# A transformer block with two layer norms on one core: a step of the second norm moved to GpSimd, two weight loads moved in the transfer queue, all work orders written anew

## The reference, cut to what matters

```
x: (4, 512, 128) fp32; 16 heads of 8; hidden width 512
qkv = x @ qkv_w.T + qkv_b            # per head: q, k, v of 8 each
attn = softmax(q @ k.T / sqrt(8)) @ v, for each batch and head
a = attn @ fc_w.T + fc_b + x
x1 = layernorm(x + a)                # (x - mean) / sqrt(var + 1e-5)
h = silu((x1 @ w1.T) * s1) * ((x1 @ w2.T) * s2)
h = gelu((h @ h1.T) * hs1);  h = gelu((h @ h2.T) * hs2)
out = layernorm(x1 + (h @ w3.T) * s3)
```

## Time and profile before

| | us |
|---|---|
| median of 3 runs | 313.34 (312.37 to 314.75) |
| the profiled execution's own time | 313.6 |
| its span, first to last instruction | 311.8 |
| busy: TensorE, VectorE | 290.1, 249.6 |
| busy: ScalarE, GpSimd | 241.4, 143.4 |

### The profile page before, as it was taken

One profiled execution on the slowest core, in us unless ns is written; L12 is line 12 of the kernel. 1 busy time (PEld: TensorE's weight loads), 2 busy tenths in 40 slices (PEclk: granted clock), 3 DMA queues, 4 the chain that ended last, 5 costly groups with the idle time before them and its releaser, 6 DMA issues.

```text
span 311.8 us, 6746 instructions
## 1 busy us (share of the span) xinstructions
PE 290.1 (93%) x2337; PEld 167.9 (54%) x2337; DVE 249.6 (80%) x561; ACT 241.4 (77%) x458; POOL 143.4 (46%) x255
## 2 busy tenths in 40 slices
PE   8959699999999999999999999998999999999991
PEld 8733254456555546353444363454556568558980
DVE  0669779998989999798899868538998784658993
ACT  2744588898979998999999888989886896984440
POOL 5162679514628991606149816707493290000101
PEclk9979899999999999999999999999999999999996
DMA  5687410045641004403610034450100000010011
GB/s 156 192 149 166 151 37 5 4 65 72 107 68 35 4 0 69 71 5 47 93 52 4 2 55 85 67 78 10 34 4 3 2 3 2 2 36 0 3 34 38
DMA packets 20276, 15.67 MB, mean 50 GB/s; under 512 B 2945, under 2 KB 19090, under 8 KB 20242
## 3 DMA queue, kind: packets, MB, share of 16 engines
q1 hardware_dynamic: 20242, 15.22, 24.9%
HBM read 5.51 MB, written 1.05 MB: 21 GB/s over the span
## 4 chain that ended last, share of the span: by engine, by line
PE 65%; DVE 12%; ACT 8%; SPq 5%; issue 4%; DMA 3%; POOL 0%; POOLq 0%; DVEq 0%; ACTq 0%
PE bank L484 23%; PE bank L524 14%; PE bank L495 8%; PE bank L506 8%; DVE negmax L879 7%; SPq L382 4%; ACT prob L735 4%; PE bank L466 2%; PE bank L548 2%; DMA stack<-mT 2%; PE bank L477 2%; DMA stack<-parts 1%; PE bank L578 1%; PE bank L459 1%; PE bank L565 1%
## 5 line engine op out<-in xcount | busy, mean ns | idle before, releaser
L879 DVE TENSOR_REDUCE negmax<-bank 128x1 f32<-128x512 f32 x256 | 159.8, 682 | 29.9 <-PE bank L495 29.4
L735 ACT ACTIVATE prob<-bank 128x512 f32<-128x512 f32 x256 | 134.0, 618 | 9.1 <-PE bank L506 8.0
L484 PE MATMUL bank<-act,hT 128*128 128x256 f32 (+1 forms) x384 | 71.0, 329 | 0.3 <-DVE negmax L879 0.2
L524 PE MATMUL bank<-prob,v_sb 128*32 128x256 f32 (+1 forms) x768 | 67.4, 458 | 1.2 <-DVE negmax L879 0.9
L484 PEld LDWEIGHTS bank<-act,hT 128*128 128x128 f32 x384 | 55.2, 189 | 11.6 <-issue 3.7
L495 PE MATMUL bank<-stack 64*128 64x512 bf16 x256 | 56.8, 385 | 4.5 <-DMA stack<-parts 3.2
L506 PE MATMUL bank<-stack 64*128 64x256 bf16 (+1 forms) x384 | 55.1, 309 | 3.6 <-DMA stack<-mT 2.8
L802 ACT ACTIVATE h_nat<-bank,hs_all 128x256 f32<-128x256 f32 (+1 forms) x48 | 25.0, 548 | 20.2 <-PE bank L484 19.9
L506 PEld LDWEIGHTS bank<-stack 64*128 64x128 bf16 x384 | 19.6, 94 | 32.1 <-issue 13.5
L524 PEld LDWEIGHTS bank<-prob,v_sb 128*32 128x32 f32 x768 | 21.7, 109 | 26.9 <-issue 16.9
L495 PEld LDWEIGHTS bank<-stack 64*128 64x128 bf16 x256 | 15.9, 94 | 34.3 <-issue 19.7
(11 more groups left out here) (119 smaller groups left out, 357.3 us busy)
## 6 DMA issues: line engine op xcount, KB each, us to landing
stack<-parts SPq DMA_DIRECT2D x64, 128.0 KB, 3.9
x_in<-in_L_attn_x_dram SPq DMA_DIRECT2D x4, 256.0 KB, 3.5
h_nat<-in_L_ffn_h_w_dram SPq DMA_DIRECT2D x1, 1024.0 KB, 7.8
work<-in_L_ffn_h_w_dram SPq DMA_DIRECT2D x1, 1024.0 KB, 6.3
res<-in_L_attn_x_dram SPq DMA_DIRECT2D x4, 256.0 KB, 3.4
work<-in_L_ffn_w_w_dram SPq DMA_DIRECT2D x2, 256.0 KB, 3.4
out_dram<-y SPq DMA_DIRECT2D x4, 128.0 KB, 2.9
out_dram<-y SPq DMA_DIRECT2D x2, 256.0 KB, 2.3
```

The source lines that it names most:

```text
L484: mm = nc.tensor.matmul(dst, w, v, start=first and n == 0, stop=last and n == len(pairs) - 1)
L524: last = nc.tensor.matmul(space("P", pfirst)[at:at + VW, 0:w], v_sb[b % 2][:, kt, of:of + VW], prob[:, t % NP, c * w:(c + 1) * w], start=k ...
L735: nc.scalar.activation(prob[:, n % NP, :], space("T", n)[:, :], ACT.Exp, scale=SCALE).then_inc(emptied("T", n), 1)
L879: nc.vector.tensor_reduce(negmax[:, g % 2, col:col + 1], space("S", n)[:, :], AX.X, ALU.max, negate=True).then_inc(emptied("S", n), 1)
```

## The change

1. `LN_STEPS` is 4: the normalization is a token of its own, `n1` or `n2`, in the function `normalize`, which either VectorE or GpSimd can run. The table `NORM` puts the second norm's normalization of units 0 to 3 on GpSimd (four `n2` tokens, 12 instructions) and leaves that of units 4 and 5, and all of the first norm, on VectorE. `x1_ok` and `y_ok` become one semaphore for each engine (`until_norm`). The residual adds get waits on them.
2. `SP_ORDER`: the second `mrow` comes right behind the batch-0 transfers; `l3` and the second `lh` follow it, instead of preceding it. `xres` of batch 0 moves behind the fifth `mrow`, `xin` of batch 2 behind the sixth. The batch-0 transfers are in another order among themselves (pair 2 completes with the sixth transfer, not the eighth, pair 4 with the thirteenth, not the tenth).
3. `PE_ORDER`: five `K` instead of nine before the first `x`; the total stays 30, and five now stand at the very end. `wt` 3 comes behind the first eight `S`, where it stood ahead of them, `wt` 5 behind the twenty-second, where it stood behind the eighth. `wt` 7 to 9 come ahead of the ninth `T`, where they came behind it, and `Y` of unit 4 comes behind the first `W` of unit 5.
4. `POOL_ORDER`: `xr` of batches 0 and 1 come later (batch 1's behind the twelfth `m`, where it stood behind the eighth), all `n2` are new. `DVE_ORDER`: the last `lo` of a batch's operands moves ahead by some tokens for batch 3; all of unit 4's second norm moves behind unit 5's last split. `r` gets a wait on `qk_lo`. A `lo` branch is added for GpSimd, but no token of `POOL_ORDER` uses it. `ACT_ORDER` follows the others.

```diff
 SP_ORDER = """
 lw lh xin vb
-zk zq zk zq*4 zk*6 mrow zq*3 l3 lh mrow xres mrow more xin mrow*2 spread mrow spread*2 xin spread mrow xres mrow*2 spread*2 mrow*2 spread*2 mrow xres
-out mrow spread*2 mrow spread*2 mrow out xres mrow*3 out*4"""
+zk zq*2 zk zq zk*3 zq zk*3 zq mrow zq*3 mrow lh l3 mrow more mrow*2 xres spread mrow xin spread xin spread*2 mrow xres mrow*2 spread*2 mrow spread
+mrow spread mrow out mrow xres spread*2 mrow spread*2 mrow out xres mrow*3 out*4"""
 PE_ORDER = """
-K:0 K:1 K:2 K:3 K:4 K:5 K:6 K:7 K:0 x:1 wq:2 q:3 q:4 K:5 wf:6 K:7 wt:0 wt:1 K:2 K:5 K:3 K:7 K:4 K:2 v:5 wt:3 K:7 x:6 wt:4 S:0 S:2 S:1 S:7 S:3 S:5 S:0
+K:0 K:1 K:2 K:3 K:4 x:5 wq:6 q:7 q:0 K:1 K:2 K:3 wt:4 K:5 K:6 wt:1 K:7 v:2 K:3 K:0 K:5 K:6 wf:7 wt:4 x:1 S:3 S:0 S:5 S:6 S:2 S:7 S:1 S:4 wt:3 wt:0 K:5
...
-H*3 X:5 K:0 H*2 H:7 A:2 A:3 B*2 H A:4 B H A:1 B H*5 H:0 H*7 H:5623 H*7 W:7 H W*3 H H:4105 H*2 Y:6 H*7 K:2 K:3 K:7 W:6 W*3 K:4 Y:1"""
+B A:5 B A:6 B H*2 A:2 H*5 H:0 B H*7 H:4715 H*8 W:3 H H:6024 W*2 H*9 W W:7 Y:1 W*3 Y:5 K:6 K:0 K:2 K:3 K:4"""
 DVE_ORDER = """
...
-gh*4 l0 gl*4 gh gl gh*2 gl*2 gh l2 gl l2*3 gh gl gh*2 gl gh gl*2 l2*7"""
+gh gl*2 gh gl*2 gh*2 gl*2 gh*2 gl*2 l2*8 n2*2"""
 POOL_ORDER = """
...
-db h0 l0 m xr gh*3 gl gh gl*3 m gh*4 gl*4 p1 m xr h0*2 l0 h0*2 l0*3 m p2 gh*3 gl gh gl*3 m p1*2 p2*3"""
+l0 h0 m h0 u l0*2 h0 l0 xr p2 n2 m gh*3 gl gh gl*3 m gh gl gh*3 gl*3 p1 m xr h0*3 l0*3 h0 l0 m gh*2 gl*2 gh*2 gl*2 m p1 p2 n2 p1 p2 n2 p2*2"""
@@ -102,7 +102,7 @@
     TWO_ONES = float(np.array([0x3F803F80], np.uint32).view(np.float32)[0])
     WT = 3 + 2 * NK
     NP = 16
-    LN_STEPS = 5
+    LN_STEPS = 4
 
     UNITS = [(0, 0, 2), (0, 2, 2), (1, 0, NT), (2, 0, NT), (3, 0, 2), (3, 2, 2)]
     NU = len(UNITS)
@@ -110,6 +110,7 @@
               4), (3, 4, 4), (3, 8, 4), (3, 12, 4), (4, 0, 8), (4, 8, 8), (5, 0, 8), (5, 8, 8)]
     GATE_DVE = {3, 4, 5}
     SPLIT0 = [0, 0, 0, 0, 1, 1]
+    NORM = [(1, 0), (1, 0), (1, 0), (1, 0), (1, 1), (1, 1)]
     SPLIT_G = [(0, 0), (0, 0), (0, 0), (0, 1), (1, 1), (1, 1)]
     DIRECT = {(4, 0), (4, 1), (5, 0), (5, 1)}
     INNER_K = {5}
@@ -139,6 +140,7 @@
     P_AFTER = [max(j for j, o in enumerate(P_OG) if o == og) + 1 for og in range(NO * NU)]
     GATE_POOL = [(u, k) for u in range(NU) if u not in GATE_DVE for k in range(NK)]
     GATE_VEC = [(u, k) for u in range(NU) if u in GATE_DVE for k in range(NK)]
+    ON_N = [[[u for u in range(NU) if NORM[u][i] == e] for e in range(2)] for i in range(2)]
     ON_0 = [[(u, k) for u in range(NU) for k in range(NK) if SPLIT0[u] == e] for e in range(2)]
     ON_G = [[(u, y, k) for u in range(NU) for y in range(2) for k in range(NK) if SPLIT_G[u][y] == e] for e in range(2)]
     H_PIECES = []
@@ -263,7 +265,7 @@
         lo_max, ps_low = sem("lo_max"), sem("ps_low")
         res2, resb = sem("res2"), sem("resb")
         rs_ok, ln_step = ([sem(f"{n}{i}") for i in range(2)] for n in ("rs_ok", "ln_step"))
-        x1_ok, y_ok = sem("x1_ok"), sem("y_ok")
+        x1_ok, y_ok = ([sem(f"{n}{e}") for e in range(2)] for n in ("x1_ok", "y_ok"))
         ps_x1T, hi_x1T = sem("ps_x1T"), sem("hi_x1T")
         ps_w1, ps_w2, ev_w1, gate_ok = (sem(n) for n in ("ps_w1", "ps_w2", "ev_w1", "gate_ok"))
         ps_h, gel_ok, parts_z, gate_t, raw_ok = (sem(n) for n in ("ps_h", "gel_ok", "parts_z", "gate_t", "raw_ok"))
@@ -350,6 +352,11 @@
         def mrow_done(g):
 
             return (mrow[g % NG], 16 * sum(m_dmas(i) for i in range(g % NG, g + 1, NG)))
+
+        def until_norm(eng, i, u):
+
+            e = NORM[u][i]
+            eng.wait_ge((x1_ok, y_ok)[i][e], ON_N[i][e].index(u) + 1)
 
         def until_0(eng, sems, u, k):
 
@@ -443,11 +450,12 @@
                     sp.dma_start(vb[:, :], qkv_b.partition_broadcast(P)).then_inc(ld_vb, 16)
                 elif what == "xres":
                     sp.wait_ge(ps_wq, 2)
-                    wait(sp, x1_ok, FIRST[n])
+                    if n:
+                        until_norm(sp, 0, FIRST[n] - 1)
                     sp.dma_start(x_res[:, :, :], x[n].rearrange("(t p) c -> p t c", p=P)).then_inc(ld_res, 16)
                 elif what == "out":
                     b, t0, nt = UNITS[n]
-                    sp.wait_ge(y_ok, n + 1)
+                    until_norm(sp, 1, n)
                     sp.dma_start(out[b, t0 * P:(t0 + nt) * P].rearrange("(t p) c -> p t c", p=P), y[:, tiles(n), :]).then_inc(st_out, 16)
             sp.wait_ge(st_out, 16 * NU)
 
@@ -579,7 +587,7 @@
                                                 fcT[:, :], start=True, stop=True)
                     last.then_inc(ps_fc, 1)
                 elif what == "X":
-                    pe.wait_ge(x1_ok, n + 1)
+                    until_norm(pe, 0, n)
                     until_free(pe, "X", n)
                     transposes(space("X", n), x1[UNITS[n][0] % 2], n).then_inc(ps_x1T, 1)
                 elif what in ("A", "B"):
@@ -677,6 +685,21 @@
                 steps(1, False)
             with pe.Else():
                 steps(2, False)
+
+        def normalize(eng, do, e, i, n):
+
+            u = ON_N[i][e][n]
+            b, t0, nt = UNITS[u]
+            eng.wait_ge(rs_ok[i], u + 1)
+            if i:
+                wait(eng, st_out, 16 * BEFORE[u])
+            elif b > 1:
+                eng.wait_ge(ps_x1T, LAST[b - 2] + 1)
+                until_empty(eng, "Y", LAST[b - 2])
+            dst, done = ((x1[b % 2], x1_ok), (y, y_ok))[i]
+            for t in range(t0, t0 + nt):
+                last = do.tensor_scalar(dst[:, t, :], res[i][:, t, :], mv[i][:, t, 0:1], rstd[i][:, 1, t:t + 1], ALU.subtract, ALU.mult)
+            last.then_inc(done[e], 1)
 
         def split_0(eng, do, e, what, n):
 
@@ -840,10 +863,13 @@
                 if k == 0 and i == 0:
                     dve.wait_ge(ps_fc, u + 1)
                     dve.wait_ge(resb, b + 1)
+                    if BEFORE[u]:
+                        until_norm(dve, 0, BEFORE[u] - 1)
                     nc.vector.tensor_tensor(flat(r), space("f", u)[:, 0:width(u)], flat(x_res), ALU.add).then_inc(emptied("f", u), 1)
                 elif k == 0:
                     dve.wait_ge(ps_w3T, u + 1)
-                    wait(dve, y_ok, BEFORE[u])
+                    if BEFORE[u]:
+                        until_norm(dve, 1, BEFORE[u] - 1)
                     nc.vector.tensor_tensor(flat(r), space("Y", u)[:, 0:width(u)], flat(x1_b), ALU.add).then_inc(emptied("Y", u), 1)
                 elif k == 1:
                     until_empty(dve, "fY"[i], u)
@@ -855,20 +881,9 @@
                     for t in ts:
                         last = nc.vector.bn_aggr(mv[i][:, t, :], stats[i][:, t, :])
                     last.then_inc(ln_step[i], 1)
-                elif k == 3:
+                else:
                     dve.wait_ge(ln_step[i], 3 * u + 2)
                     nc.vector.tensor_scalar(rstd[i][:, 0, tiles(u)], mv[i][:, tiles(u), 1], EPS, None, ALU.add).then_inc(ln_step[i], 1)
-                else:
-                    dve.wait_ge(rs_ok[i], u + 1)
-                    if i:
-                        wait(dve, st_out, 16 * BEFORE[u])
-                    elif b > 1:
-                        dve.wait_ge(ps_x1T, LAST[b - 2] + 1)
-                    dst, done = ((x1_b, x1_ok), (y, y_ok))[i]
-                    for t in ts:
-                        last = nc.vector.tensor_scalar(dst[:, t, :], r[:, t, :], mv[i][:, t, 0:1], rstd[i][:, 1, t:t + 1],
-                                                       ALU.subtract, ALU.mult)
-                    last.then_inc(done, 1)
 
             for what, n, _ in walk(DVE_ORDER):
                 if what == "s":
@@ -881,6 +896,8 @@
                 elif what == "r":
                     i = 1 - n % 2
                     dve.wait_ge(qk_hi, n + 1)
+                    if n > 3:
+                        dve.wait_ge(qk_lo, n - 3)
                     nc.vector.scalar_tensor_tensor(qk_r[i][:, :], space("q", n)[:, :], qkb[:, i:i + 1], parts[i][:, 0, :],
                                                    ALU.add, ALU.subtract).then_inc(emptied("q", n), 1)
                 elif what == "mid":
@@ -926,6 +943,8 @@
                         h0 = GH * (PO * o + j)
                         last = nc.vector.tensor_tensor(attn[:, tiles(u), HD * h0:HD * (h0 + GH)].rearrange("p t (c d) -> p t c d", d=HD), sums, den, ALU.mult)
                     last.then_inc(emptied("o", n), 1)
+                elif what in ("n1", "n2"):
+                    normalize(dve, nc.vector, 1, int(what == "n2"), n)
                 elif what in ("l1", "l2"):
                     layernorm(n % LN_STEPS, n // LN_STEPS, int(what == "l2"))
                 elif what == "Xh":
@@ -1000,6 +1019,8 @@
                         nc.gpsimd.memset(v_sb[n][:, :, 0:H * VC].rearrange("p t (o h w) -> p t o h w", o=NO, w=VC)[:, :, :, GH * j:GH * (j + 1), at:at + 1], 1.0).then_inc(vzero, 1)
                     if n == 1:
                         nc.gpsimd.memset(mhalf[:, :], -0.5).then_inc(vzero, 1)
```

(7 more changed lines are left out.)

60 lines of the change are left out of this document (30 added, 30 removed).

## The result

| | before | after |
|---|---|---|
| median of 19 runs, us | 313.59 (312.36 to 316.56) | 311.19 (309.60 to 314.04) |
| ratio after/before, 95% interval | | 0.9926 (0.9903 to 0.9948) |
| profiled execution, us | 313.60 | 310.37 |
| its span, us | 311.8 | 308.4 |
| its busy time: TensorE, VectorE, GpSimd, us | 290.1, 249.6, 143.4 | 291.3, 246.8, 155.9 |

The kernel became 2.4 us faster; 4.6 were forecast (313.34 to 308.7). The time lies inside the range, between its middle and its upper end. It is a gain of under 1%; a change of less than 1% either way had a chance of 0.28.

The account below looks back on a forecast made before the run. TensorE was taken to bound most of the kernel (93% busy, 65% of the chain). 313.6 - 4.3 (start) - 0.3 (n2), other terms 0, gave 309.0; 0.26 above the median, so 308.7. Range 305.8 to 312.2; own range 306 to 310.8.

Parts of the forecast that it names:

- Part 7: All other order changes in the engines' lists: no sign readable, so 0, ends -2.5 and +2.5 us.
- A: Rival at the start: the h2 and w3 loads move the stall to the third maxima row; 311.4 us, chance 0.14.
- C: Rival: n2 steps on GpSimd block VectorE steps for their own length, half on the path; 311.4 us, chance 0.04.
- Four fewer fillers: TensorE before the first transposition: sixteen zero matmuls of 0.055 us go; ends 0 and 0.9 us, 0.6 taken.
- The second maxima row: SyncE, second mrow ahead of the h2 and w3 loads: wait ends 5.0 us earlier, fillers included; VectorE sets the stretch.
- Parts 1 and 2: Fewer fillers and the earlier second maxima row together: 4.3 us gain taken, bounds 1.8 and 5.0.
- xres and xin later: SyncE's residual and input loads issued later: covers of 2.3 and about 2 us stay, cost 0.
- n2 on GpSimd: Twelve second-norm steps leave VectorE (3.5 us busy time), 0.45 us each on GpSimd; -0.3 us, ends +1.0 and -1.0.
- Batch-3 operands: VectorE's last lo comes two maxima and an o step earlier; TensorE had work there: 0, with -1.0 us as an end.
- The tail: Unit 4's second norm behind unit 5's last split, where VectorE waits anyway: cost 0, upper end 0.5 us.
- B: Rival: later xr and added n2 make GpSimd late, kernel slower; 319.6 us, or 314 if the loss is halved; chance 0.10.
- D: Rival: fillers' gain lost in the full DMA queue, row's gain given back at the first batch boundary; 313 us, chance 0.04.

Follow-up runs that it names:

- start71: Changed kernel's orders up to about 71 us, the kernel before's orders from there on, second norms on VectorE: 308.90 us, ratio 0.9848 to the kernel before.
- start112b: Changed orders up to about 112 us (GpSimd's queue to about 150 us), the kernel before's behind, second norms on VectorE: 312.91 us, ratio 1.0002.
- fill_back: start71 with four fillers (16 zero matmuls) put back ahead of the first transposition: 311.46 us, ratio 0.9927 to the kernel before.
- fill_fewer: start71 with four more fillers taken away ahead of the first transposition (30 zero matmuls, not 46): 307.70 us, ratio 0.9841 to the kernel before.
- n2_only: Kernel before with only the second norm's last step of the first four units moved to GpSimd: 315.17 us, ratio 1.0049.
- row_only: Kernel before with only the second maxima row's issue moved ahead of the h2 and w3 loads on SyncE: 311.84 us, ratio 0.9928.
- row_wt: row_only with the TensorE transposition that needs the h2 load moved five tokens later: 313.44 us, ratio 1.0001 to the kernel before.
- start112: Changed kernel's orders up to about 112 us, the kernel before's from there on, second norms on VectorE: 309.99 us, ratio 0.9902.

## Why the prediction missed

**The forecast was wrong in size, by one term.** Part 7, the rest of the orders, stood at 0 with ends of -2.5 and +2.5, for "a badly placed token costs about half such a wait". It was +3.3 in the profiled execution (5.45 down to 2.12), and +2.3 by the medians of start71 and the changed kernel. The working priced one token and had no reason for the 0 but that no sign could be read. What was moved was the whole list of five engines: start112b shows 4.8 us for a list of one queue that does not go with the others. start71, the new start without the rest, came to 308.9, where 308.7 was written for the whole. The range beside the sum was too narrow for its own terms: part 7 at its upper end alone gives 308.7 + 2.5 = 311.2, the measured median, and "306 to 310.8" leaves it out.

1. *Four fewer fillers.* Right: 5.09 us for 46 zero matmuls, which end at 6.06 where 6.0 was named, and 0.85 to 1.03 us for sixteen. In fill_back all of it counts, not 0.6. The two clock levels were read from the pitch of the matmuls; the granted clock in the earlier trace rows is 1.00 in both stretches and doesn't show them. That those at the slower pitch always come first holds, but how many they are is a matter of the execution, as fill_fewer shows.
2. *The second maxima row.* Right in mechanism. Issue at 26.43 (26.7 written), no idle on VectorE, clock up, 32nd maximum at 38.1 (near 39 written). Parts 1 and 2 were put at 4.3 with an upper bound of 5.0; 5.4 came in the profiled execution, 4.7 by start71's median. Two things lie between. VectorE's 16th maximum was already 1.3 us earlier, where I had only the fillers' 0.6, and the stall of the one execution of before was a long one (n2_only).
3. *xres and xin later.* GpSimd now waits 7.7 us for residual loads, 3.3 before, but the first residual add does not wait for it. Cost 0, as written.
4. *n2 on GpSimd.* VectorE's busy time fell by 2.8 us where 3.5 was written. A step cost 0.79 us (1.12 where it comes first behind a power step), not 0.45, and GpSimd gained 12.5 us of busy time, 10.1 of them n2:

```profile
L701 POOL TENSOR_SCALAR y<-res,mv,rstd 128x128 f32<-128x128 f32 x12 | 10.1, 848 | 0.3
```

5. *Batch-3 operands.* Not tested apart. The last `lo` began 5.9 us earlier and ended 4.9 us earlier, since it took 1.67 us where 0.68 is usual. It runs beside a `tensor_tensor` of GpSimd's (1.28 us) and the first `xr` step, which took 1.49 in place of 1.04:

```profile
175.42 1.28 POOL L718 TENSOR_TENSOR act<-work,act 128x512 fp32r<-128x512 f32 x1
175.59 1.67 DVE L910 TENSOR_TENSOR parts<-qk_r,parts 128x512 bf16<-128x512 f32 x1
176.66 1.49 POOL L1079 TENSOR_TENSOR res<-res 128x512 f32<-128x512 f32 x1
...
177.91 0.39 PE L514 MATMUL bank<-stack 64*128 64x512 bf16 x1 [0.63 <-DVE negmax L894]
```

TensorE waits 0.63 us for VectorE right behind it. But the advance falls by only 0.4 us from step 537 to 659, so the new collision is at most that part of the 1.2 us lost behind 166 us.

6. *The tail.* Right that it costs nothing: the last power step is at 304.76 with 0.73 us, 2.2 earlier like all before it (4 to 5 were written, with the forecast's whole gain).
7. *The rest.* The failed step, above.

**The rivals.** A's number, 311.4, is nearest to the time, but its wait is in row_only and row_wt, not in the changed kernel. The range 305.8 to 312.2 was drawn wide enough to take in A and C, and that it holds the result is luck: neither's mechanism made the time. B's wait was shown in start112, at 3.1 us, and not in the change: GpSimd's fourteenth `m` began 5.5 us earlier, at 182.9 (188 was named as the sign), and VectorE never waits for `y`. C, in part: VectorE was held up there, but by the copies, which before had as well, and not by n2. The Trainium skill ("SBUF — State Buffer", "Who interferes with whom") says that `tensor_scalar` on VectorE in a two-port mode and a GpSimd instruction block each other for the whole instruction. Beside the copies of 0.61 us the trace agrees, with 0.64 a tile; beside n2 steps of 0.80 us it does not, with 0.34 to 0.48 a tile. D had the right shape (the gain given back), but named transfers at a batch boundary, and TensorE waited 3.0 us for operand transfers in all, 3.2 before.

**What stays open.** That the rest of the orders is what costs is shown by start71; which tokens cost it is shown for a small part only. Of the 2.1 us up to 166 us, 0.6 to 0.7 are the collision. The other 1.4 or so, and the 1.2 behind, are not separated by any run here; TensorE's waits there are of 0.2 to 1.0 us each.
